# Macaron block, softmax attention: the causal mask moved from VectorE's minima to TensorE

## The chip, the cores and the metric

The kernel runs on one NeuronCore of one Trainium2 chip. The metric is the device time of one execution in microseconds (us), the median of several runs. One further execution was recorded by the hardware profiler, and all rows below come from it. A NeuronCore has TensorE (PE in the rows; PEld is its weight load), VectorE (DVE), ScalarE (ACT), GpSimd (POOL) and SyncE (SP), each with a queue of its own; they wait for each other by semaphores. TensorE writes only into PSUM, here eight banks of 512 fp32 columns over 128 partitions.

## What is computed

Two layers on x of shape (4, 1024, 128), each a half-weighted feed-forward part, an attention part and the feed-forward part again. The change touches the second layer's attention:

```python
D_K = 64
Q = jnp.einsum('bmd,hdk->bhmk', x, P_q)          # 16 heads
K = jnp.einsum('bmd,hdk->bhmk', x, P_k)
V = jnp.einsum('bmd,hdv->bhmv', x, P_v)
logits = jnp.einsum('bhmk,bhnk->bhmn', Q, K) * math.sqrt(D_K)
causal = jnp.tril(jnp.ones((m, m), dtype=bool))
logits = jnp.where(causal[None, None], logits, -jnp.inf)
key_weights = jax.nn.softmax(logits, axis=-1)
o = jnp.einsum('bhmm,bhmv->bhmv', key_weights, V)
y = jnp.einsum('bhmv,hdv->bmd', o, P_o)
```

The einsum with `mm` takes the diagonal of the weights alone. So for each head and query the kernel needs the masked row's extreme, the sum of the exponentials over the row, and the logit of the query with its own key.

## The kernel before

The program is a row of stages, each with its own code for the five engines. The stage here is `softmax_diagonal`. It runs over 32 units: unit `u` is head pair `u % 8` in batch `u // 8`. A unit has the scores of two heads, 1024 queries by up to 1024 keys. Queries go in eight tiles of 128; tile `q` needs keys 0 to `(q + 1) * 128` (`wide(q)`), so only its last 128 columns cross the diagonal. The tiles run in the order 1, 5, 6, 4, 2 (with 0), 3, 7 (`ORDER`, `LITTLE`).

**TensorE.** Q and K are split into a high and a low part, and each score is the sum of three products (`passes`). Head 0 of the pair lies on partitions 0 to 63, head 1 on 64 to 127, so a score matmul uses 64 rows of the array (`64*128` in the rows), and two of them, one for each head, can run beside each other. `big` (L2830) does the tiles of 640 to 1024 keys: for each head two halves of the keys in two banks, six matmuls a head, head 1's issued two steps behind head 0's (`SKEW`). `little` (L2855) does tiles 1, 2, 0 and 3 with one bank for a head. `diagonals` (L2845) sums the products of each query with its own key, with 128 rows and 32 columns of the array. `project` (L2808 to L2810) makes Q and K of the next unit, three matmuls of 128 rows for each of four halves; it stands ahead of tile 1 of the unit. The eight banks go round in order (`first_bank`); before a bank is written again, `wait_bank` waits until its last reader is done. So tile 4 waits for the exps of tile 5, tile 7 for those of tile 4.

**VectorE.** `lowest` (L2962) adds the mask to a tile's scores in PSUM, stores them back and takes their minimum (the scores are negated by the scale of -1 that the exp has) into `arg`, one instruction for each head and tile, each followed by a short one that reads the accumulator. It also copies Q's and K's second halves out of PSUM (`copy_out_dve`, L2891), adds up the diagonals (`add_own`), and at batch ends inverts, divides and copies (`invert`, `divide`, `keep`).

**ScalarE.** `exps` (L2942) does exp with the minimum as bias in place in PSUM and accumulates the sum; it also copies the first halves of Q and K (L2885).

**GpSimd** splits the copies into high and low parts and multiplies Q by K for the diagonals.

Semaphores: `scored` counts finished heads of tiles, `mx_done` minima, `exp_done` exps.

Of the kernel before, what the change touches and what calls it, by code (L numbers as in the profile page):

```python
# [17 lines left out]
BF16 = mybir.dt.bfloat16  # L18
I32 = mybir.dt.int32
U32 = mybir.dt.uint32  # L20
ALU = mybir.AluOpType
# [81 lines left out]
def build(nc, I, out):  # L103
# [41 lines left out]
    ident = sb("ident", [P, P], F32)  # L145
    before = sb("before", [P, P], BF16)
    onesb = sb("onesb", [P, P], BF16)
    cmask = sb("cmask", [P, SEQ], BF16)
    pair_ones = sb("pair_ones", [P, 3 * H1], F32)
    iota = sb("iota", [P, 32], F32)  # L150
    sel32 = sb("sel32", [P, E0], F32)
# [203 lines left out]
    def setup():  # L355
# [45 lines left out]
        def gpsimd(pool):  # L401
# [18 lines left out]
            select(before[:], [[1, P]], 0, -1, ALU.is_gt, 0.0)  # L420
            pool.memset(onesb[:], 1.0)
            then(pool.memset(cmask[:], 0.0))
            select(cmask[:, SEQ - P:], [[-1, P]], 0, 1, ALU.is_ge, MASKED)
            then(pool.memset(pair_ones[:], 0.0))
            then(pool.memset(pair_ones[:, H1:H1 + 2], 1.0))
            select(pair_ones[:, H1:H1 + 1], [[0, 1]], DK - 1, -1, ALU.is_ge, 0.0)
# [2229 lines left out]
    def softmax_diagonal(split, used):  # L2656
# [68 lines left out]
        def wait_bank(pe, k, freed, count):  # L2725

            if k in last_user:
                pe.wait_ge(*last_user[k])
            last_user[k] = (S[freed], count)

        def out_count(v, kind, half):
            mine = [k for k, h in PROJECT if h == half]
            return v * len(mine) + mine.index(kind) + 1

        def wait_out(pool, v, kind):

            pool.wait_ge(S["out_act"], out_count(v, kind, 0))
            pool.wait_ge(S["out_dve"], out_count(v, kind, 1))

        def copy_of(v, kind, half):  # L2740
            return (KF[v % 2] if kind == "k" else QF)[:, half * BLK:(half + 1) * BLK]
# [39 lines left out]
                project(pe, 1, k)  # L2781

        def open_out(pe):
            pe.wait_ge(S["out_act"], out_count(0, "q", 0))
            pe.wait_ge(S["out_dve"], out_count(0, "k", 1))

        def open_act(act):
            copy_out_act(act, 0)
# [10 lines left out]
        def project(pe, v, k):  # L2799
            kind, half = PROJECT[k]  # L2800
            g, b = which(v)
            wh, wl = (all_w[:, 2 * (kind == "k") + w, g * P:(g + 1) * P] for w in range(2))
            at = slice(b * SEQ + half * BLK, b * SEQ + (half + 1) * BLK)
            to = project_bank(v, k)
            if k == 0 and v < 2:
                pe.wait_ge(split["xl_done"], 2 if v == 0 else 4)
            wait_bank(pe, to, "out_dve" if half else "out_act", out_count(v, kind, half))
            pe.matmul(bank(to), wh, xl[:, at], start=True, stop=False)  # L2808
            pe.matmul(bank(to), wl, xh[:, at], start=False, stop=False)  # L2809
            pe.matmul(bank(to), wh, xh[:, at], start=False, stop=True).then_inc(S["projected"], 1)  # L2810

        def tensor(pe):
# [4 lines left out]
            def head(w, a, at, n):  # L2817
                return w[a * DK:(a + 1) * DK, at:at + n]

            def big(u, n):  # L2820
                q = ORDER[n]
                half = wide(q) // 2
                steps = [(p, k) for p in range(3) for k in range(2)]

                def step(a, m):
                    p, k = steps[m]
                    qs, ks = passes(u)[p]
                    if p == 0:
                        wait_bank(pe, (first_bank(u, n) + 2 * a + k) % BANKS, "exp_done", scored_before(u, n, a) + 1)
                    last = pe.matmul(big_scores(u, n, a)[:, k, :], head(qs, a, q * P, P),  # L2830
                                     head(ks, a, k * half, half), start=(p == 0), stop=(p == 2))
                    if m == len(steps) - 1:
                        last.then_inc(S["scored"], 1)

                for m in range(len(steps) + SKEW):
                    if m < len(steps):
                        step(0, m)
                    if m >= SKEW:
                        step(1, m - SKEW)
# [8 lines left out]

            def little(u, n):
                for a in range(2):  # L2850
                    wait_bank(pe, (first_bank(u, n) + a) % BANKS, "exp_done", scored_before(u, n, a) + 1)
                for q in LITTLE[ORDER[n]]:
                    for p, (qs, ks) in enumerate(passes(u)):
                        for a in range(2):
                            last = pe.matmul(small_scores(u, n, q, a), head(qs, a, q * P, P), head(ks, a, 0, wide(q)),  # L2855
                                             start=(p == 0), stop=(p == 2))
                            if p == 2 and q == LITTLE[ORDER[n]][-1] and q != DIAG:
                                last.then_inc(S["scored"], 1)
                if ORDER[n] == DIAG:
                    g, b = which(u)  # L2860
                    if g == 0 and b > 0:
                        last = turn_own(pe, b - 1, spare_of(u, 0))
                    last.then_inc(S["scored"], 1)
                    diagonals(u)
# [15 lines left out]

        def copy_out_act(act, v):
            for k, (kind, half) in enumerate(PROJECT):
                if half == 0:
                    wait_copy(act, v, k, kind)
                    act.activation(copy_of(v, kind, half), bank(project_bank(v, k)), ACT.Copy).then_inc(S["out_act"], 1)  # L2885

        def copy_out_dve(dve, v):
            for k, (kind, half) in enumerate(PROJECT):
                if half == 1:
                    wait_copy(dve, v, k, kind)  # L2890
                    dve.tensor_copy(copy_of(v, kind, half), bank(project_bank(v, k))).then_inc(S["out_dve"], 1)  # L2891

# [65 lines left out]
                        last.then_inc(S["exp_done"], 1)  # L2958
        def vector(dve):
            def lowest(u, q, a, src):  # L2960
                mask = cmask[:, SEQ - wide(q):].rearrange("p (k n) -> p k n", k=src.shape[1])
                return dve.tensor_tensor_reduce(src, src, mask, 1.0, 3e38, ALU.add, ALU.min, kept_at(arg, u, q, a))  # L2962

            def add_own(u):
                g, b = which(u)
# [9 lines left out]
            for u in range(UNITS):  # L2975
                if u < UNITS - 1:
                    copy_out_dve(dve, u + 1)
                for n, q in enumerate(ORDER):
                    done = u // PAIRS - 1
                    if done >= 0 and n == 1 and u % PAIRS == 0:  # L2980
                        invert(dve, done)
                    if done >= 0 and n == 1 and u % PAIRS == 1:
                        divide(dve, done)
                    if done >= 0 and n == 3 and u % PAIRS == 1:
                        keep(dve, done)
                    for a in range(2):
                        dve.wait_ge(S["scored"], scored_before(u, n, a) + 1)
                        if q == DIAG and a == 0 and u > 0 and u % PAIRS == 0:
                            arguments(dve, u // PAIRS - 1, spare_of(u, 0))
                        if q == DIAG and a == 1:  # L2990
                            add_own(u)
                        if q >= BT:
                            last = lowest(u, q, a, big_scores(u, n, a))
                        else:
                            for one in LITTLE[q]:
                                last = lowest(u, one, a, small_scores(u, n, one, a).unsqueeze(1))
                        last.then_inc(S["mx_done"], 1)

        opening = Opening(open_pe, open_act, open_dve, open_out, next_pe)
        closing = Beside(end_pe, end_act, end_dve)  # L3000
# [134 lines left out]
```

## Time and profile before

| | us |
|---|---|
| median of 3 runs (1689.14 to 1694.79) | 1689.76 |
| profiled execution | 1692.65 |
| its span, first to last instruction | 1690.5 |
| busy in it: TensorE | 1469.8 |
| VectorE | 1335.7 |
| ScalarE | 1022.8 |
| GpSimd | 861.6 |

Busy time is the union of an engine's instructions. Matmuls overlap each other in their pipeline, and the ends of matmuls are modelled, so distances between starts tell more of TensorE than durations. The chain of work that ended last is followed back from the last instruction, at each step to what released it; its rows give start, length and number of instructions. A timeline row gives start, length, engine, line, operation, output <- inputs with shapes, the number of instructions merged, and in brackets the idle time before it and what ended it.

### The profile page before, as it was taken

What the parts mean: (1) busy time and instruction counts of PE and PEld (TensorE: products, weight loads), DVE (VectorE), ACT (ScalarE), POOL (GpSimd) and SP (SyncE); (2) the same over time, 40 slices, a digit from 0 to 9 for tenths busy, and PEclk for the clock granted to TensorE, in tenths of its full rate; (3) what the DMA queues carried; (4) which work ended last, traced back from release to release, by engine and by line L of the source; (5) the groups of instructions that cost most, each with busy time, mean ns of one, the idle gap of its engine ahead of it and who ended that gap; (6) DMA issues with size and microseconds to landing.
All of it is one profiled execution on the core that took longest, in us unless ns stands there. A gap on an engine that the chain in (4) does not pass through costs nothing.

```text
span 1690.5 us, 30128 instructions
## 1 busy us (share of the span) xinstructions
PE 1469.8 (87%) x8653; PEld 1074.6 (64%) x8653; DVE 1335.7 (79%) x3816; ACT 1022.8 (61%) x2170; POOL 861.6 (51%) x743
## 2 busy tenths in 40 slices
PE   5999999898999994999549999999989899769990
PEld 4778877655666663777436676667666566457770
DVE  7599998567667675787679999999989767857876
ACT  7444432364223234888569999989989622268880
POOL 5756653210134333577656666656656225637673
PEclk9999998999999996999869999999989999879995
DMA  9990010000101004232199800000000001122225
GB/s 194 178 182 17 1 24 28 1 1 1 30 31 45 31 18 100 54 79 67 43 205 181 150 1 1 2 1 1 1 1 1 1 15 36 41 56 68 68 63 150
DMA packets 182171, 91.67 MB, mean 54 GB/s; under 512 B 43829, under 2 KB 176902, under 8 KB 182048
## 3 DMA queue, kind: packets, MB, share of 16 engines
q1 hardware_dynamic: 167840, 71.19, 23.1%
q0 software_dynamic: 9984, 16.89, 3.1%
q10 hardware_dynamic: 4224, 2.10, 0.4%
q8 instruction: 60, 0.98, 0.2%
q14 instruction: 63, 0.52, 0.1%
HBM read 32.59 MB, written 61.18 MB: 55 GB/s over the span
## 4 chain that ended last, share of the span: by engine, by line
PE 63%; DVE 14%; ACT 8%; issue 6%; DMA 3%; POOL 3%; DVEq 2%; SPq 1%; POOLq 0%; ACTq 0%
PE psum L1362 9%; PE psum L2830 7%; PE psum L658 5%; PE psum L2855 5%; PE psum L659 4%; PE psum L660 4%; ACT psum L2942 4%; DVE psum L2962 3%; PE psum L2808 2%; PE psum L2809 2%; PE psum L2810 2%; PE psum L1121 1%; PE psum L190 1%; PE psum L1123 1%; PE psum L1122 1%
## 5 line engine op out<-in xcount | busy, mean ns | idle before, releaser
L2942 ACT ACTIVATE psum<-psum,gate 128x128 f32<-128x128 f32 (+7 forms) x512 | 368.1, 727 | 39.8 <-DVE gate L2962 37.9
L2962 DVE CUSTOM_DVE_ANT_0 psum<-psum,cmask 128x128 f32<-128x128 f32 (+7 forms) x512 | 371.3, 790 | 16.3 <-PE psum L2830 11.7
L2440 POOL DMA_INDIRECT answers<-ed,answer_to x184 | 202.5, 1101 | 80.2 <-issue 43.7
L1362 PE MATMUL psum<-raw_all,w 128*128 128x512 f32 x384 | 195.4, 592 | 1.5 <-DVE raw_all L1490 1.5
L658 PE MATMUL psum<-xl,wreg 128*128 128x512 f32 x320 | 182.0, 569 | 2.8 <-ACT psum L2942 1.5
L1488 DVE SCALAR_TENSOR_TENSOR raw_all<-psum,hg 128x512 f32<-128x512 f32 x128 | 88.1, 690 | 67.3 <-PE psum L660 64.5
L2830 PE MATMUL psum<-spare_sets_room 64*128 64x384 f32 (+3 forms) x768 | 115.3, 369 | 16.2 <-ACT psum L2942 16.2
L659 PE MATMUL psum<-xh,wreg 128*128 128x512 f32 x320 | 126.9, 396 | 0.0
L660 PE MATMUL psum<-xh,wreg 128*128 128x512 f32 x320 | 126.5, 395 | 0.0
L2830 PE MATMUL psum<-hh,hl 64*128 64x384 f32 (+3 forms) x768 | 113.1, 376 | 13.4 <-ACT psum L2942 13.4
L2830 PEld LDWEIGHTS psum<-spare_sets_room 64*128 64x128 f32 x768 | 85.9, 185 | 45.3 <-ACT psum L2942 39.3
L2830 PEld LDWEIGHTS psum<-hh,hl 64*128 64x128 f32 x768 | 87.9, 194 | 39.0 <-ACT psum L2942 32.3
L2356 DVE TENSOR_TENSOR hl<-gate,hh 128x512 fp32r<-128x512 f32 x92 | 63.4, 690 | 59.3 <-ACT hh L2318 36.9
L2942 ACT ACTIVATION_READ_ACCUMULATOR psum<-psum,gate 128x1 f32 x512 | 110.2, 215 | 0.0
L1235 POOL TENSOR_TENSOR hl<-hg,hh 128x512 fp32r<-128x512 f32 x65 | 85.9, 1324 | 47.5 <-ACT hh L1167 46.6
L819 POOL DMA_INDIRECT rows<-raw_all,row_no x64 | 61.7, 965 | 78.5 <-PE psum L660 63.8
L819 POOL DMA_INDIRECT rows<-row,row_no x64 | 62.0, 968 | 69.1 <-PE psum L660 52.1
L1167 ACT ACTIVATE hh<-hg 128x512 fp32r<-128x512 f32 x86 | 54.1, 633 | 67.1 <-DVE hg L1198 65.2
L201 POOL TENSOR_TENSOR spare_p<-spare_p 128x1 f32<-128x1 f32 x63 | 19.5, 309 | 134.6 <-DVE row_no L780 64.0
L658 PEld LDWEIGHTS psum<-xl,wreg 128*128 128x128 f32 x320 | 61.3, 192 | 39.2 <-issue 27.6
L1362 PEld LDWEIGHTS psum<-raw_all,w 128*128 128x128 f32 x384 | 72.1, 189 | 19.9 <-DVE raw_all L1490 2.1
L659 PEld LDWEIGHTS psum<-xh,wreg 128*128 128x128 f32 x320 | 61.5, 192 | 32.2 <-issue 27.7
(432 smaller groups left out, 4073.3 us busy)
## 6 DMA issues: line engine op xcount, KB each, us to landing
rows<-blank SPq DMA_DIRECT2D x146, 258.0 KB, 7.3
row<-rows SPq DMA_DIRECT2D x46, 256.0 KB
raw_all<-answers SPq DMA_DIRECT2D x32, 256.0 KB, 4.7
w<-in_L_ffn_W_dram SPq DMA_DIRECT2D x16, 256.0 KB, 3.1
answers<-ed,answer_to POOLq DMA_INDIRECT x184
x<-in_L_attn_x_dram SPq DMA_DIRECT2D x4, 512.0 KB, 6.1
out_dram<-x ACTq DMA_DIRECT2D x8, 256.0 KB, 4.7
rawD<-in_L_ffn_values_dram SPq DMA_DIRECT2D x4, 256.0 KB, 6.9
```

Of the source, the lines that this page charges most:

```text
L658: pe.matmul(dst, wh, xl[:, blk(i)], start=start, stop=False)
L659: pe.matmul(dst, wl, xh[:, blk(i)], start=False, stop=False)
L660: return pe.matmul(dst, wh, xh[:, blk(i)], start=False, stop=stop)
L819: pool.indirect_dma_start(rows, bass.IndirectOffsetOnAxis(ap=row_no[:, i % 2, c, t:t + 1], axis=0), row_of(i)[:, t, c, :], None).then_inc( ...
L1235: pool.tensor_tensor(hl[:, j % SLOTS, :], kept[n % len(kept)], hh[:, j % SLOTS, :].bitcast(F32), ALU.subtract).then_inc(S["lo_pool"], 1)
L1362: pe.matmul(bank(B_OUT[i % 2]), col(dn, j), hidden[:, n % HID, :], start=(j == 0), stop=(j == nf - 1)).then_inc(S["dn_done"], 1)
L1488: last = dve.scalar_tensor_tensor(out, raw, 0.0, gates_now, ALU.max, ALU.mult)
L2440: pool.indirect_dma_start(answers, bass.IndirectOffsetOnAxis(ap=answer_to[:, out.odd, t:t + 1], axis=0), y_row[:, out.odd, t, :], None, bo ...
L2830: last = pe.matmul(big_scores(u, n, a)[:, k, :], head(qs, a, q * P, P), head(ks, a, k * half, half), start=(p == 0), stop=(p == 2))
L2855: last = pe.matmul(small_scores(u, n, q, a), head(qs, a, q * P, P), head(ks, a, 0, wide(q)), start=(p == 0), stop=(p == 2))
L2942: return act.activation(src, src, ACT.Exp, bias=kept_at(arg, u, q, a), scale=-1.0, accum_out=kept_at(esum, u, q, a))
L2962: return dve.tensor_tensor_reduce(src, src, mask, 1.0, 3e38, ALU.add, ALU.min, kept_at(arg, u, q, a))
```

## The change

The mask becomes a 128x128 bf16 tile, and a bf16 identity `ident16` is made beside it. TensorE adds the mask: `hide` multiplies the identity by the mask and accumulates into the 128 diagonal columns of the scores, ahead of the last matmul that writes there. That is once for each head and tile, 16 times a unit, with all 128 rows of the array. VectorE's `lowest` becomes a plain minimum that writes nothing back; for tiles 1, 2, 0 and 3 one instruction (`lowest_two`) takes the minima of both heads, after waiting for both. Three of the four halves of Q and K are copied by VectorE, and K's first half alone by ScalarE (`BY_ACT`). Waits follow: `wait_bank` is given the semaphore itself, and `wait_out` waits for both halves.

```diff
-    cmask = sb("cmask", [P, SEQ], BF16)
+    cmask = sb("cmask", [P, P], BF16)
+    ident16 = sb("ident16", [P, P], BF16)
...
-            select(cmask[:, SEQ - P:], [[-1, P]], 0, 1, ALU.is_ge, MASKED)
+            select(cmask[:], [[-1, P]], 0, 1, ALU.is_ge, MASKED)
+            then(pool.tensor_copy(ident16[:], ident[:]))
...
+        BY_ACT = (("k", 0),)
+
+        def out_sem(kind, half):
+            return S["out_act" if (kind, half) in BY_ACT else "out_dve"]
...
-            pool.wait_ge(S["out_act"], out_count(v, kind, 0))
-            pool.wait_ge(S["out_dve"], out_count(v, kind, 1))
+            for half in range(2):
+                e.wait_ge(out_sem(kind, half), out_count(v, kind, half))
...
+            def hide(diagonal):
+
+                pe.matmul(diagonal, ident16[:], cmask[:], start=False, stop=False, skip_group_check=True)
+
             def big(u, n):
...
                     qs, ks = passes(u)[p]
+                    if (p, k) == (2, 1):
+                        hide(big_scores(u, n, a)[:, 1, half - P:half])
...
                     for p, (qs, ks) in enumerate(passes(u)):
+                        if p == 2:
+                            for a in range(2):
+                                hide(small_scores(u, n, q, a)[:, wide(q) - P:])
                         for a in range(2):
...
-                if half == 0:
+                if (kind, half) in BY_ACT:
...
             def lowest(u, q, a, src):
-                mask = cmask[:, SEQ - wide(q):].rearrange("p (k n) -> p k n", k=src.shape[1])
-                return dve.tensor_tensor_reduce(src, src, mask, 1.0, 3e38, ALU.add, ALU.min, kept_at(arg, u, q, a))
+                return dve.tensor_reduce(kept_at(arg, u, q, a), src, AX.XY, ALU.min)
+
+            def lowest_two(u, n, q):
+                g, b = which(u)
+                at = 3 * P if q == 0 else 0
+                src = psum[:, first_bank(u, n):first_bank(u, n) + 2, at:at + wide(q)]
+                return dve.tensor_reduce(arg[:, b * QT + q, 2 * g:2 * g + 2], src, AX.X, ALU.min)
...
-                    for a in range(2):
-                        dve.wait_ge(S["scored"], scored_before(u, n, a) + 1)
-                        if q == DIAG and a == 0 and u > 0 and u % PAIRS == 0:
-                            arguments(dve, u // PAIRS - 1, spare_of(u, 0))
-                        if q == DIAG and a == 1:
-                            add_own(u)
-                        if q >= BT:
-                            last = lowest(u, q, a, big_scores(u, n, a))
-                        else:
-                            for one in LITTLE[q]:
-                                last = lowest(u, one, a, small_scores(u, n, one, a).unsqueeze(1))
-                        last.then_inc(S["mx_done"], 1)
+                    if q >= BT:
+                        for a in range(2):
+                            dve.wait_ge(S["scored"], scored_before(u, n, a) + 1)
+                            lowest(u, q, a, big_scores(u, n, a)).then_inc(S["mx_done"], 1)
+                        continue
+                    dve.wait_ge(S["scored"], scored_before(u, n, 0) + 1)
+                    if q == DIAG and u > 0 and u % PAIRS == 0:
+                        arguments(dve, u // PAIRS - 1, spare_of(u, 0))
+                    dve.wait_ge(S["scored"], scored_before(u, n, 1) + 1)
+                    if q == DIAG:
+                        add_own(u)
+                    for one in LITTLE[q]:
+                        last = lowest_two(u, n, one)
+                    last.then_inc(S["mx_done"], 2)
```

On TensorE's queue, tile 1, the diagonals and tiles 5, 6 and 4 of one unit stood so in the kernel before (the name, the output and inputs, and the output's shape; L2855 is `little`, L2845 the diagonals, L2830 `big`):

```order
L2855 MATMUL psum<-hh,hl 128x256 x6
L2845 MATMUL psum<-ed,pair_ones 32x256 x4
L2830 MATMUL psum<-hh,hl 128x384 x12
L2830 MATMUL psum<-hh,hl 128x448 x12
L2830 MATMUL psum<-hh,hl 128x320 x12
```

And tile 1, the diagonals and tiles 5 and 6 in the changed kernel, where L2829 is `hide`, L2871 `little`, L2858 the diagonals and L2843 `big`:

```order
L2871 MATMUL psum<-hh,hl 128x256 x4
L2829 MATMUL psum<-cmask,ident 128x128 x2
L2871 MATMUL psum<-hh,hl 128x256 x2
L2858 MATMUL psum<-ed,pair_ones 32x256 x4
L2843 MATMUL psum<-hh,hl 128x384 x8
L2829 MATMUL psum<-cmask,ident 128x128
L2843 MATMUL psum<-hh,hl 128x384 x3
L2829 MATMUL psum<-cmask,ident 128x128
L2843 MATMUL psum<-hh,hl 128x384
L2843 MATMUL psum<-hh,hl 128x448 x8
L2829 MATMUL psum<-cmask,ident 128x128
L2843 MATMUL psum<-hh,hl 128x448 x3
```

In the narrow tile the two mask products stand together ahead of the last pair; in a wide tile they stand after eight and after eleven of the twelve score matmuls.

On VectorE's queue, from the copies to tile 5, one unit before (ISA is the masked minimum, with its accumulator read behind it):

```order
L2891 COPY hg<-psum 128x512
L2891 COPY row<-psum 128x512
L2962 ISA psum,gate<-psum,cmask 128x256
L2962 ISA gate 128x1
L2972 TENSOR_TENSOR own<-psum,own 128x256
L2962 ISA psum,gate<-psum,cmask 128x256
L2962 ISA gate 128x1
L2962 ISA psum,gate<-psum,cmask 128x2x384
```

And in the changed kernel the whole turn of a unit:

```order
L2907 COPY hg<-psum 128x512
L2907 COPY row<-psum 128x512
L2907 COPY hg<-psum 128x512
L2993 TENSOR_TENSOR own<-psum,own 128x256
L2983 TENSOR_REDUCE gate<-psum 128x2
L2977 TENSOR_REDUCE gate<-psum 128x1 x6
L2983 TENSOR_REDUCE gate<-psum 128x2 x3
L2977 TENSOR_REDUCE gate<-psum 128x1 x2
```

A third copy stands ahead of the minima, the diagonals' sum goes ahead of tile 1's minimum, and tile 1 has one minimum in place of two.

## Rows read from the trace of the kernel before

**Rows 1.** The page, chain that ended last, by engine.
```profile
PE 63%; DVE 14%; ACT 8%; issue 6%; DMA 3%; POOL 3%; DVEq 2%; SPq 1%; POOLq 0%; ACTq 0%
```
**Rows 2.** Busy by stretch: length, PE, PEld, DVE, ACT, POOL, clock, DMA, GB/s.
```profile
1054.30:1068.07 13.77, 12.90 (x97) 9.57 (x93) 13.25 (x36) 12.87 (x36) 9.15 (x5) 1.00 0.01 2
885.00:1325.00 440.00, 406.90 (x2853) 304.40 (x2849) 419.22 (x1094) 400.11 (x1054) 282.41 (x155) 0.97 0.21 33
```
**Rows 3.** The chain in one unit: start us, us, what.
```profile
1054.37 1.25 PE psum L2830 x12
...
1055.64 0.97 DVE psum L2962
...
1056.70 1.91 ACT psum L2942 x4
...
1058.66 1.14 PE psum L2830 x9
...
1064.08 0.43 PE psum L2808
...
1067.02 0.55 PE psum L2855 x6
...
1068.13 0.37 PE psum L2830
```
**Rows 4.** Timeline of TensorE, tile 4's first matmuls, a unit earlier.
```profile
1043.97 0.70 PE L2830 MATMUL psum<-spare_sets_room 64*128 64x320 f32 x3 [0.55 <-ACT psum L2942]
```
**Rows 5.** Timeline of TensorE around changes of form.
```profile
1052.63 0.39 PE L2809 MATMUL psum<-xh,wreg 128*128 128x512 f32 x1
1052.86 0.39 PE L2810 MATMUL psum<-xh,wreg 128*128 128x512 f32 x1
1053.18 0.39 PE L2855 MATMUL psum<-hh,hl 64*128 64x256 f32 x2
...
1053.52 0.28 PE L2855 MATMUL psum<-hh,hl 64*128 64x256 f32 x2
1053.73 0.41 PE L2845 MATMUL psum<-ed,pair_ones 128*32 128x256 f32 x2
...
1063.70 0.38 PE L2830 MATMUL psum<-hh,hl 64*128 64x512 f32 x1
1064.01 0.50 PE L2808 MATMUL psum<-xl,wreg 128*128 128x512 f32 x1
```
**Rows 6.** VectorE by line and shape: count, busy us, mean ns, idle before.
```profile
L2962 DVE DVE_READ_ACCUMULATOR2_ANT gate<- 128x1 f32 x512 | 72.1, 141 | 0.0
L2962 DVE CUSTOM_DVE_ANT_0 psum<-psum,cmask 128x512 f32<-128x512 f32 x64 | 44.1, 731 | 0.0
L2891 DVE COPY hg<-psum 128x512 f32<-128x512 f32 x31 | 21.2, 685 | 0.0
...
L1794 DVE TENSOR_REDUCE k_sum<-raw_all 128x64 f32<-128x512 f32 x8 | 5.5, 686 | 0.5
L847 DVE TENSOR_REDUCE hg<-hg 128x32 f32<-128x256 f32 x2 | 0.8, 420 | 0.1
```
**Rows 7.** Timeline of VectorE, tile 7's two minima.
```profile
1050.16 1.26 DVE L2962 CUSTOM_DVE_ANT_0 psum<-psum,cmask 128x1024 f32<-128x1024 f32 x1
...
1051.34 1.26 DVE L2962 CUSTOM_DVE_ANT_0 psum<-psum,cmask 128x1024 f32<-128x1024 f32 x1
```
**Rows 8.** Timeline of TensorE in a later stage, bf16 matmuls and a load.
```profile
1403.35 0.10 PEld L1394 LDWEIGHTS psum<-m,onesb 128*128 128x128 bf16 x1 [0.33 <-issue]
...
1403.35 0.19 PE L1394 MATMUL psum<-m,before 128*128 128x64 bf16 x1
1403.38 0.20 PE L1394 MATMUL psum<-m,onesb 128*128 128x64 bf16 x1
```
**Rows 9.** The chain around a batch end: tile 5 of four units.
```profile
982.44 1.25 PE psum L2830 x12
...
1026.83 1.25 PE psum L2830 x12
```

More of the change, by code:

```diff
@@ L2728, in wait_bank, with wait_out @@
                 pe.wait_ge(*last_user[k])
-            last_user[k] = (S[freed], count)
+            last_user[k] = (freed, count)
+        BY_ACT = (("k", 0),)
+        def out_sem(kind, half):
+            return S["out_act" if (kind, half) in BY_ACT else "out_dve"]
         def out_count(v, kind, half):
-            mine = [k for k, h in PROJECT if h == half]
-            return v * len(mine) + mine.index(kind) + 1
-        def wait_out(pool, v, kind):
-            pool.wait_ge(S["out_act"], out_count(v, kind, 0))
-            pool.wait_ge(S["out_dve"], out_count(v, kind, 1))
+            mine = [one for one in PROJECT if (one in BY_ACT) == ((kind, half) in BY_ACT)]
+            return v * len(mine) + mine.index((kind, half)) + 1
+        def wait_out(e, v, kind):
+            for half in range(2):
+                e.wait_ge(out_sem(kind, half), out_count(v, kind, half))
         def copy_of(v, kind, half):
@@ L2783, in open_out @@
         def open_out(pe):
-            pe.wait_ge(S["out_act"], out_count(0, "q", 0))
-            pe.wait_ge(S["out_dve"], out_count(0, "k", 1))
+            wait_out(pe, 0, "k")
+            wait_out(pe, 0, "q")
         def open_act(act):
@@ L2806, in project @@
                 pe.wait_ge(split["xl_done"], 2 if v == 0 else 4)
-            wait_bank(pe, to, "out_dve" if half else "out_act", out_count(v, kind, half))
+            wait_bank(pe, to, out_sem(kind, half), out_count(v, kind, half))
             pe.matmul(bank(to), wh, xl[:, at], start=True, stop=False)
@@ L2827, in step @@
                     qs, ks = passes(u)[p]
+                    if (p, k) == (2, 1):
+                        hide(big_scores(u, n, a)[:, 1, half - P:half])
                     if p == 0:
-                        wait_bank(pe, (first_bank(u, n) + 2 * a + k) % BANKS, "exp_done", scored_before(u, n, a) + 1)
+                        wait_bank(pe, (first_bank(u, n) + 2 * a + k) % BANKS, S["exp_done"], scored_before(u, n, a) + 1)
                     last = pe.matmul(big_scores(u, n, a)[:, k, :], head(qs, a, q * P, P),
@@ L2850, in little @@
                 for a in range(2):
-                    wait_bank(pe, (first_bank(u, n) + a) % BANKS, "exp_done", scored_before(u, n, a) + 1)
+                    wait_bank(pe, (first_bank(u, n) + a) % BANKS, S["exp_done"], scored_before(u, n, a) + 1)
                 for q in LITTLE[ORDER[n]]:
                     for p, (qs, ks) in enumerate(passes(u)):
+                        if p == 2:
+                            for a in range(2):
+                                hide(small_scores(u, n, q, a)[:, wide(q) - P:])
                         for a in range(2):
@@ L2888, in copy_out_dve @@
             for k, (kind, half) in enumerate(PROJECT):
-                if half == 1:
+                if (kind, half) not in BY_ACT:
                     wait_copy(dve, v, k, kind)
```

## The prediction

> **What bounds the kernel now.** I read the page first, then the busy time of the engines in the softmax stage, then the chain of work that ended last in one unit, then TensorE's single matmuls. The page gives TensorE 63% of the chain and VectorE 14% [rows 1], too coarse to judge one stage. The stage that the change edits runs from about 885 to 1325 us: 32 units (head pair times batch) in which TensorE is busy 407 of 440 us, VectorE 419 and ScalarE 400 [rows 2]. Three engines look full at once, so the busy shares don't tell which one sets the time.
>
> The chain over one unit does [rows 3]: 384-wide halves of query tile 5 on TensorE (1.25 us), VectorE's minimum (0.97), ScalarE's exps of both heads (1.91), then TensorE alone: from 1058.66 tile 4, tiles 2, 0, 3 and tile 7, from 1064.08 to 1067.02 twelve projection matmuls, then tile 1, the diagonals, and at 1068.13 tile 5 of the next unit. From tile 5 to tile 5 (1054.37 to 1068.13) a unit lasts 13.76 us. Only tile 6 is off the chain, since TensorE runs it while VectorE and ScalarE work on tile 5. About 10.8 of the 13.8 us of the chain are TensorE's (13.76 less 0.97 and 1.91, and 0.1 between them). VectorE itself is at 13.25 of 13.77 us [rows 2]. So the chain and VectorE's own queue are nearly the same length, and anything put on TensorE outside tile 6 lengthens the chain at once.
>
> How much could TensorE take? Tile 4's matmuls wait for the exps of tile 5: three start after 0.55 us of idle time (1043.97, a unit of 13.77 earlier; so 1057.74 here) [rows 4], and the other nine at 1058.66 [rows 3]. Summing TensorE without waits: projections 2.94, tile 1 and the diagonals 1.11 (1067.02 to 1068.13), tile 5 1.15 (its 1.25 less the modelled end) [rows 3]; the others at 0.23 us per 512 columns (1052.63 to 1052.86 [rows 5]), the two heads side by side: tile 6 1.2, tile 4 0.87, tiles 2, 0 and 3 0.52, 0.33 and 0.69, tile 7 1.38, and 0.1 before the next projections: 10.3 us. So TensorE stands idle or half used for about 3.5 us of a unit.
>
> **The change, part by part.**
>
> (a) *VectorE's wide tiles* lose the added mask and the store. The custom instruction takes 1.26 us for 1024 elements [rows 7] and 731 ns for 512 [rows 6], about 200 ns plus 1.04 ns an element. A plain reduction isn't shown at these shapes from PSUM; the nearest rows are 686 ns for 512 and 420 for 256 elements in SBUF, so about 155 plus 1.04 [rows 6]. That is 45 ns less, eight times a unit: 0.36 us. Bounds: nothing saved, to 0.14 us each if the accumulator read behind each one (141 ns [rows 6]) was never overlapped; it mostly is, and I take 45.
>
> (b) *Narrow tiles*: eight instructions become four of double width. The elements stay; 8 x 0.20 less 4 x 0.155 is 0.98 us, less the 0.08 by which neighbours overlap (1050.16 to 1051.34 is 1.18 us for an instruction of 1.26 [rows 7]), four times: about 0.65.
>
> (c) *Copies*: VectorE takes the third one, 685 ns less the overlap, so 0.6 us more [rows 6, 7]; ScalarE loses about as much. Together VectorE goes from 13.3 to about 12.9 us a unit, ScalarE from 12.9 to 12.3. If VectorE alone set the pace the stage would gain 0.4 x 32 = 13 us.
>
> (d) *The mask on TensorE*: 16 matmuls of 128 columns a unit. The columns alone are small: bf16 matmuls of 64 columns start 0.03 us apart on this clock [rows 8], so 0.055 for 128. But the scores are computed in 64-row halves (64*128 in the rows), two heads beside each other, and the identity product needs all 128 rows. The rows show what it costs to pass between these forms. Within the projections a start follows a start by 0.23 us; from the last projection (1052.86) to the first 64-row matmul (1053.18) it is 0.32; tile 7's last matmul to the next projection 1063.70 to 1064.01, 0.31. Tile 1 (256 columns, 0.115) to the diagonals (128*32) is 1053.52 to 1053.73, 0.21 [rows 5]. So 0.09 us at each change of form, while 128*128 matmuls of different lines pass without it. On top, the first matmul after a change shows its weight load: 0.39 against 0.28 us for the same 256 columns [rows 5], so 0.11. The identity's load is bf16; such a load takes 0.10 us [rows 8], and the two bf16 matmuls, each with its own, start 0.03 apart: I take 0.03 of it as exposed.
>
> One identity product between 64-row matmuls therefore costs 0.09 + 0.03 + 0.055 + 0.09 + 0.11 = 0.37 us. In the wide tiles both products of a tile stand apart: 8 x 0.37 = 3.0 us. In the narrow ones the two stand together, 0.43 a pair, four pairs: 1.7.
>
> The Trainium skill states both sides of this. TensorEngine Tiling, section Key Properties: changing the tiling mode drains the engine; the trace agrees, with the 0.09 us. TensorE: Matmul & The Clock Gate, section Back-to-back issue gap, gives about 81 ns for a 128-column matmul with its load in a stream, and by that the sixteen would be an estimated 1.3 us a unit; that is the first rival below in another form.
>
> (e) *The order in the wide tiles.* Today the two heads' six matmuls each run side by side: twelve in 1.25 us [rows 3] are six pitches of 0.17. In the new order head 0's product comes when head 1 has issued three of six, and nothing passes a full-array product. Head 1 then runs two matmuls alone: eight pitches in place of six. Two pitches more are 0.35, 0.41, 0.29 and 0.47 us for tiles 5, 6, 4 and 7: 1.5 us.
>
> (f) *Waits.* The narrow minimum now waits for both heads, so ScalarE's exp of head 0 starts later; for tile 1 also behind the diagonals. Behind this wait on VectorE stands tile 5's minimum, and VectorE has 0.5 us of a unit to spare today [rows 2]. In the new timing the wait lies under TensorE's work. Removing the store has no price. The set-up on GpSimd gets one copy and a shorter fill; it is under 1 us of 1690 and I take it as nothing.
>
> **Sum.** TensorE without waits: 10.3 + 3.0 + 1.7 + 1.5 = 16.5 us a unit. Does it then still wait? From head 0's end in tile 5 to tile 4's start TensorE has 0.17 + 0.37 + 0.17 of tile 5 and 8 x 0.2 + 0.74 of tile 6: 3.05 us. The way through VectorE and ScalarE takes 2.1 (1055.64 to 1057.74 [rows 3, 4]). So the wait for the exps is gone, and TensorE's own work is the bound. I find no other wait over 0.2 us. The unit goes from 13.77 to about 16.5, so 2.73 x 32 = 87 us. Against it: at each of three batch ends VectorE's extra work (reciprocal, division, a copy) now makes three units last 44.4 us (982.44 to 1026.83 [rows 9]) where 41.3 are regular, 3.1 more; with VectorE 3.6 us below TensorE most of it hides, and I take back 7 of the 9 us. Net +80 us. The profiled execution took 1692.65 us, 1690.5 of it span; its 2.15 us around the span stay. It lies 2.9 above the median of 1689.76; I add the 80 to the median: **1770 us**.
>
> **Rivals.**
>
> *1. The products stream without the change of form.* Each costs its columns or its load, 0.055 to 0.11 us. For it: no row shows a single full-array product between halves. Against it: the 0.09 at every change. TensorE's sum is then 10.3 + 1.5 + 0.9 to 1.8, 12.7 to 13.6, under a unit. The chain holds 14 of the 16 (all but tile 6's), so it grows by 0.8 to 1.5 us, of which VectorE's relief and the remaining waits give part back: +0.3 to +0.9 a unit, 10 to 29 us: 1700 to 1719. Chance 0.09.
>
> *2. The drain overlaps partly*, say half of the 0.31 us that isn't columns: a product costs 0.2, a pair 0.26; TensorE needs 10.3 + 1.6 + 1.0 + 1.5 = 14.4, and the chain, which waits again, about 15.2: +1.1 to +1.5 a unit less 5, so 1720 to 1735. Chance 0.09.
>
> *3. Not slower.* The products fall into TensorE's 3.5 idle us and the unit follows VectorE, 0.4 shorter: 1690 - 13 = 1677, or 1690 where the chain holds its 13.76. It decides below a price that the chain doesn't feel: 14 products cost as little as what (a) and the shared minimum take off the chain, about 0.2 us, so under 0.02 us each, less than their own columns. For it only the idle time; against it that this lies at tile 4 and the products elsewhere. Chance 0.04 (0.02 faster, 0.02 within).
>
> *4. Worse than the sum.* The granted clock is 0.97 over the stage [rows 2]; stretches at half clock partly hide in waits today and would not then; pairs may also expose a second load. Plus 0.5 to 1 us a unit: 1786 to 1802. Chance 0.13.
>
> **Numbers.** Forecast (1750 to 1786) 0.65, rivals 0.09, 0.09, 0.04, 0.13. The range 1725 to 1800 leaves out rivals 1 and 3 and the edges of 2 and 4. A measurement of this kernel tells 0.3% (5 us) from no change: faster 0.02, within 0.3% 0.02, slower 0.96.
>
> **What would show it.** Right: a unit of about 16.5 us in the chain; TensorE nearly the whole chain of the stage, with no wait for ScalarE before tile 4; each identity product starting about 0.2 us after its predecessor's start plus columns, and the next 64-row matmul showing a long first load; tile 7 lasting about 2.6 us; VectorE idle for over 3 us a unit, waiting for scores; reductions of 1024 elements near 1.22 us. Wrong: products 0.06 to 0.1 us apart from their neighbours (rival 1); VectorE still full at a unit of 16 us, which would mean that a reduction from PSUM costs far more than one from SBUF; ScalarE's exps of tile 1 late enough to hold tile 6.

## The result and the profile after

| | before | changed |
|---|---|---|
| median, us (4 runs each) | 1691.71 (1689.14 to 1694.79) | 1781.13 (1765.77 to 1781.97) |
| ratio, 95% interval | | 1.0506 (1.0446 to 1.0567) |
| span of the profiled execution, us | 1690.5 | 1779.2 |
| busy TensorE, VectorE, ScalarE, us | 1469.8, 1335.7, 1022.8 | 1589.1, 1335.5, 1011.1 |

The change costs 5.1%: 1781 us against a forecast of 1770 and a range of 1725 to 1800. (The kernel before has one run more in this table than in the one ahead of the forecast.)

The busy time of the engines in the changed kernel, first in one regular unit from tile 1 to tile 1, then over the stage; the columns are those of [rows 2]:

```profile
1054.51:1070.73 16.22, 16.22 (x109) 10.36 (x109) 13.11 (x16) 11.69 (x31) 9.01 (x5) 1.00 0.01 2
880.00:1411.00 531.00, 529.38 (x3343) 335.17 (x3339) 420.22 (x507) 388.87 (x1024) 281.74 (x155) 0.94 0.17 28
```

TensorE is busy the whole 16.22 us. VectorE's 13.11 here is about what it had in [rows 2], though its busy share is now 81%: it has room, and the room buys nothing. The chain of work that ended last says the same; here are some parts of one unit (start us, us, what; L2871 is `little`, L2829 the mask products, L2858 the diagonals, L2843 `big`):

```profile
1055.54 0.57 PE psum L2858 x8
1056.11 1.09 PE psum L2843 x7
...
1058.07 1.21 PE psum L2843 x9
...
1071.77 0.57 PE psum L2858 x8
```

No VectorE or ScalarE row stands between the two rows of the diagonals, where [rows 3] has 0.97 and 1.91 us of them. Diagonals to diagonals is 16.23 us.

TensorE's timeline from tile 5 to tile 4 of that unit shows where it goes:

```profile
1056.04 1.16 PE L2843 MATMUL psum<-hh,hl 64*128 64x384 f32 x8
1057.13 0.23 PE L2829 MATMUL psum<-cmask,ident 128*128 128x128 bf16 x1
1057.29 0.62 PE L2843 MATMUL psum<-hh,hl 64*128 64x384 f32 x3
1057.84 0.23 PE L2829 MATMUL psum<-cmask,ident 128*128 128x128 bf16 x1
1058.00 1.28 PE L2843 MATMUL psum<-hh,hl 64*128 64x384 f32 x9
1059.22 0.23 PE L2829 MATMUL psum<-cmask,ident 128*128 128x128 bf16 x1
...
1060.14 1.25 PE L2843 MATMUL psum<-hh,hl 64*128 64x448 f32 x9
1061.32 0.23 PE L2829 MATMUL psum<-cmask,ident 128*128 128x128 bf16 x1
```

From product to product in tile 5 is 0.71 us and holds two pitches of 0.175 (a pitch is the distance from one score matmul to the next that doesn't run beside it); what is left, 0.36 us, is the price of one product with the change of form to it and back. Product to next matmul is 0.16 (1057.13 to 1057.29, 1057.84 to 1058.00). The single matmuls of this trace give the other two parts: from the lone matmul at 1056.86 to the product at 1057.13 is 0.27 us, 0.09 over its pitch, and from the first matmul behind the product (1057.29) to the next (1057.57) is 0.28, 0.11 over it. The three parts are 0.09, 0.16 and 0.11; the forecast had 0.09, 0.175 and 0.11.

VectorE's reductions, by line and shape (columns as in [rows 6]):

```profile
L2977 DVE TENSOR_REDUCE gate<-psum 128x1 f32<-128x1024 f32 x64 | 75.7, 1221 | 17.8 <-PE psum L2843 17.3
L2983 DVE TENSOR_REDUCE gate<-psum 128x2 f32<-128x512 f32 x32 | 21.8, 680 | 0.0
L2993 DVE TENSOR_TENSOR own<-psum,own 128x256 f32<-128x256 f32 x28 | 11.9, 425 | 25.2 <-PE psum L2858 25.2
```

1221 ns for 1024 elements and 680 for 512: a plain reduction from PSUM costs what [rows 6] gave for SBUF, 686 ns for 512 and, by their slope, 1.22 us for 1024. The idle time ahead of the diagonals' sum (25.2 us) is VectorE waiting for TensorE.

### The profile page after: what moved, and what is told of

Its sections match the earlier page's. It is cut to its first block, busy times and chain, and to the rows that moved or that the text cites. A ratio compares the mean times of both kernels' runs of the same rounds, so it can differ in the third digit from the quotient of the medians.

```text
span 1779.2 us, 30579 instructions
## 1 busy us (share of the span) xinstructions
PE 1589.1 (89%) x9165; PEld 1100.7 (62%) x9165; DVE 1335.5 (75%) x3208; ACT 1011.1 (57%) x2138; POOL 861.8 (48%) x744
## 4 chain that ended last, share of the span: by engine, by line
PE 73%; DVE 8%; issue 5%; DMA 5%; ACT 4%; POOL 3%; SPq 1%; DVEq 0%; POOLq 0%; ACTq 0%
PE psum L2843 14%; PE psum L1364 9%; PE psum L2871 5%; PE psum L660 4%; PE psum L661 4%; PE psum L662 4%; PE psum L2829 4%; PE psum L2815 2%; DMA answers<-ed,answer_to 2%; PE psum L2816 2%; PE psum L2817 2%; PE psum L2266 2%; PE psum L2268 2%; PE psum L2267 2%; DMA row<-rows 1%
## 5 line engine op out<-in xcount | busy, mean ns | idle before, releaser
L2977 DVE TENSOR_REDUCE gate<-psum 128x1 f32<-128x768 f32 (+3 forms) x256 | 249.4, 1019 | 42.8 <-PE psum L2843 41.5
L2843 PE MATMUL psum<-spare_sets_room 64*128 64x384 f32 (+3 forms) x768 | 145.1, 403 | 1.6 <-ACT psum L2958 1.6
L2843 PE MATMUL psum<-hh,hl 64*128 64x384 f32 (+3 forms) x768 | 140.8, 399 | 0.0
L1490 DVE SCALAR_TENSOR_TENSOR raw_all<-psum,hg 128x512 f32<-128x512 f32 x128 | 88.1, 690 | 66.5 <-PE psum L662 63.8
L2983 DVE TENSOR_REDUCE gate<-psum 128x2 f32<-128x512 f32 (+3 forms) x128 | 99.7, 818 | 29.6 <-PE psum L2871 29.6
L2958 ACT ACTIVATION_READ_ACCUMULATOR psum<-psum,gate 128x1 f32 x512 | 105.6, 206 | 0.0
L2829 PEld LDWEIGHTS psum<-cmask,ident 128*128 128x128 bf16 x512 | 39.4, 97 | 103.3 <-issue 96.6
L2843 PEld LDWEIGHTS psum<-spare_sets_room 64*128 64x128 f32 x768 | 85.9, 192 | 24.5 <-issue 6.2
L2829 PE MATMUL psum<-cmask,ident 128*128 128x128 bf16 x512 | 97.5, 232 | 0.0
L2843 PEld LDWEIGHTS psum<-hh,hl 64*128 64x128 f32 x768 | 84.2, 191 | 21.2 <-issue 6.6
```

What stands on the lines that cost most here:

```text
L2829: pe.matmul(diagonal, ident16[:], cmask[:], start=False, stop=False, skip_group_check=True)
L2958: return act.activation(src, src, ACT.Exp, bias=kept_at(arg, u, q, a), scale=-1.0, accum_out=kept_at(esum, u, q, a))
L2977: return dve.tensor_reduce(kept_at(arg, u, q, a), src, AX.XY, ALU.min)
L2983: return dve.tensor_reduce(arg[:, b * QT + q, 2 * g:2 * g + 2], src, AX.X, ALU.min)
```

## Experiments

The experiments ran on chips on which the kernel before took 1706.5 us (e1 to e4) and 1710.7 us (e5 to e8), so they are compared by their ratio to it. A unit is measured in the chain from diagonals to diagonals.

### e1: the changed kernel without the mask products

```diff
             def hide(diagonal):
-                pe.matmul(diagonal, ident16[:], cmask[:], start=False, stop=False, skip_group_check=True)
+                return
```

> The changed kernel without its sixteen mask products (the mask is left out of the computation; all else of the change stays: plain minima, two heads in one narrow minimum, three copies on VectorE). My theory, that the products are the whole loss: a unit returns to 13.4 to 13.8 us and the time to 1677 to 1692 us, since VectorE's relief of about 0.4 us a unit counts only while the chain lets it. Rival, that the plain reductions from PSUM, the third copy or the wait for both heads cost something of their own: the time stays above 1700 us.

Ratio 0.9971 (0.9937 to 1.0005), 1702.5 us. Two regular units in its chain:

```profile
940.15 0.57 PE psum L2858 x8
...
953.84 0.57 PE psum L2858 x8
```

13.69 us a unit, 0.08 less than before. So the whole loss of a regular unit comes with the products, and plain minima, shared narrow minima and the third copy, which take 0.4 us a unit from VectorE, give back 0.08. The first theory holds by the unit; the rival that VectorE's part costs something there falls. In time, 1702.5 against 1706.5 us is at the edge of what the runs can tell. It is above the 1692 that I named as the upper end, and above the rival's 1700 too, but so is the kernel before on this chip; times the 1691.7 us of the first chip the ratio gives 1687. At the batch ends VectorE's part isn't free: the second unit after each lasts 18.5 us here, where two of the three in the trace of the kernel before last 15.4 and 15.5.

### e2: the kernel before with the products and nothing else

```diff
+                    if (p, k) == (2, 1):
+                        hide(big_scores(u, n, a)[:, 1, half - P:half])
...
+                        if p == 2:
+                            for a in range(2):
+                                hide(small_scores(u, n, q, a)[:, wide(q) - P:])
```

> The kernel before with the sixteen identity products added and nothing else of the change (VectorE adds the mask once more, which leaves the result as it is). My theory: TensorE sets the time and VectorE's work doesn't matter, so a unit is 16.2 us as in the changed kernel and the time 1770 to 1790 us. Rival, that the changed VectorE work has a part in the loss: the time is nearer to 1740 us. Rival, that VectorE's relief hides a part of the products' cost: it is above 1795 us.

Ratio 1.0529 (1.0511 to 1.0546), 1796.0 us. That is the changed kernel's own ratio within its interval, reached without any of its VectorE work. Busy time in 80 us of regular units:

```profile
920.00:1000.00 80.00, 80.00 (x533) 50.96 (x531) 66.51 (x174) 65.21 (x168) 43.10 (x25) 1.00 0.66 109
```

TensorE 80.00 of 80, VectorE 66.5. The absolute time lies above the 1770 to 1790 that I named, and 1 us above the second rival's 1795; the kernel before is 0.9% slower on this chip too, and times the first chip's 1691.7 the ratio gives 1781. A regular unit is 16.34 us in this trace, 0.11 more than in the changed kernel. So the second rival is right in kind but small: VectorE's relief hides about 0.1 us of a unit, as in e1, some 3 us of the kernel. e1 and e2 together leave the products as the cause of the loss.

### e3: heads in step, both products of a tile together

```diff
-        SKEW = 2
+        SKEW = 0
...
-                    if (p, k) == (2, 1):
-                        hide(big_scores(u, n, a)[:, 1, half - P:half])
+                    if (p, k) == (2, 1) and a == 0:
+                        for one in range(2):
+                            hide(big_scores(u, n, one)[:, 1, half - P:half])
```

> The changed kernel with the two heads of a wide tile issued in step (SKEW 0) and both mask products together ahead of the last pair: eight changes of form fewer, and no matmul that runs alone. By my sum TensorE needs 10.3 + 8 x 0.43 = 13.7 us a unit in place of 16.5; then the chain through VectorE and ScalarE binds again with seven of the eight pairs of products on it (13.76 + 3.0 less 0.3 to 1.5): 15.3 to 16.3 us a unit, 1735 to 1770 us. Rival, that the products cost by their number and not by where they stand: no change from 1781 us.

Ratio 1.0399 (1.0378 to 1.0421), 1774.4 us, with the same sixteen products. A unit is 15.90 us:

```profile
951.67 0.57 PE psum L2859 x8
...
967.57 0.55 PE psum L2859 x5
```

That is inside 15.3 to 16.3; in time 1774 is 4 us over what I named, on the slower chip. Against e2, on the same chip, it gains 22 us: about 13 in the regular units and 9 in the first unit of the stage, which lasts 17.4 us here and 26.6 there, with the granted clock at 0.50 for 6.8 and for 27.3 us. TensorE's timeline at tiles 6 and 4 shows that the bound has moved back to the exps:

```profile
1072.12 0.28 PE L2829 MATMUL psum<-cmask,ident 128*128 128x128 bf16 x2
1072.33 0.70 PE L2844 MATMUL psum<-spare_sets_room 64*128 64x448 f32 x3
1073.49 0.99 PE L2844 MATMUL psum<-spare_sets_room 64*128 64x320 f32 x9 [0.47 <-ACT psum L2959]
```

The pair costs 0.21 us from its first product to the next matmul, against 0.16 for a lone one, so the second product adds 0.05. TensorE now waits 0.47 us before tile 4. The products on the chain cost even where TensorE has time to spare elsewhere; where they stand matters, but not enough.

### e4: the mask in the 64-row form

Each product is split into two of 64 rows on the partitions of its head, so that no change of form is left within the scores. `ident2` and `cmask2` hold the other half's rows.

```diff
+            then(pool.memset(ident2[:], 0.0))
+            select(ident2[:], [[-1, P]], DK, 1, ALU.not_equal, 1.0)
+            select(ident2[:], [[-1, P]], -DK, 1, ALU.not_equal, 1.0)
+            then(pool.memset(cmask2[:], MASKED))
+            select(cmask2[:], [[0, P]], -DK, 1, ALU.is_ge, 0.0)
+            select(cmask2[:], [[1, P]], DK, -1, ALU.is_gt, 0.0)
+            select(cmask2[:], [[-1, P]], DK, 1, ALU.is_ge, MASKED)
...
-            def hide(diagonal):
-                pe.matmul(diagonal, ident16[:], cmask[:], start=False, stop=False, skip_group_check=True)
+            def hide(diagonal, a):
+                rows = slice(a * DK, (a + 1) * DK)
+                for one, mask in ((ident16, cmask), (ident2, cmask2)):
+                    pe.matmul(diagonal, one[rows, :], mask[rows, :], start=False, stop=False, skip_group_check=True)
```

> The changed kernel with each mask product split in two of 64 rows each, on the partitions of its head, so that TensorE never leaves the 64-row form within the scores: 32 products in place of 16, in the places of before. My theory, that the change of form and the order that it forces are the cost: a unit falls from 16.24 to 14.0 to 14.4 us, the time to 1695 to 1712 us. Rival, that a product costs by its number, its bf16 type or its write into PSUM: twice as many cost at least as much, 1781 us or more.

Ratio 1.0073 (1.0050 to 1.0096), 1718.8 us: 32 products in place of 16 cost 0.7% in place of 5.1%. (1718.8 is over the 1695 to 1712 that I named; times the first chip's 1691.7 the ratio gives 1704.) The unit in its chain, and tile 7's products in its timeline (L2839 the products, L2853 `big`):

```profile
947.55 0.57 PE psum L2868 x8
...
961.92 0.57 PE psum L2868 x8
```

```profile
1059.82 0.39 PE L2853 MATMUL psum<-spare_sets_room 64*128 64x512 f32 x1
1059.82 0.28 PE L2839 MATMUL psum<-cmask,ident 64*128 64x128 bf16 x2
1059.92 0.53 PE L2853 MATMUL psum<-spare_sets_room 64*128 64x512 f32 x2
```

14.37 us a unit, inside 14.0 to 14.4. The two products start together with the other head's score matmul and the next one follows 0.10 us later. The rival (cost by number, by type or by the write into PSUM) falls: twice the products, a seventh of the loss. What is left against e1, 0.68 us a unit, lies in tiles 5, 2, 3 and 1, by the starts of the tiles in the two traces: 0.16 to 0.19 us each. Tiles 6, 4, 0 and 7 with the projections behind them are no longer than in e1, or by 0.02 us at most.

### e7: each product of the wide tiles twice

```diff
-                        hide(big_scores(u, n, a)[:, 1, half - P:half])
+                        for _ in range(2):
+                            hide(big_scores(u, n, a)[:, 1, half - P:half])
```

> The changed kernel with each mask product of the wide tiles issued twice in a row (masked scores get the mask twice, the result is the same): eight products a unit more, no change of form more. My theory, that of a product's 0.36 us only 0.055 are its columns and the rest the two changes of form: a unit grows by 0.45 to 0.6 us, from 16.24 to 16.7 to 16.85. Rival, that each product costs 0.3 us or more wherever it stands: 18.6 us and over.

This kernel ran once, in 1800.5 us, and wasn't timed beside the others, so only its unit counts:

```profile
1085.56 0.57 PE psum L2859 x8
...
1102.08 0.57 PE psum L2859 x8
```

16.52 us, 0.29 more for eight products, less than the 0.45 to 0.6 I named and far from 18.6. In the timeline the second product adds the 0.05 us expected (1103.65 to 1103.86 is 0.21):

```profile
1103.65 0.28 PE L2829 MATMUL psum<-cmask,ident 128*128 128x128 bf16 x2
1103.86 0.62 PE L2844 MATMUL psum<-hh,hl 64*128 64x384 f32 x3
```

Eight times 0.05 would be 0.4. The rest is a wait that it fills, in tile 4. From its first matmul to its first product are 1.18 us in the changed kernel (1060.14 to 1061.32 above) and 1.01 here:

```profile
1106.88 1.08 PE L2844 MATMUL psum<-hh,hl 64*128 64x448 f32 x9
1107.89 0.29 PE L2829 MATMUL psum<-cmask,ident 128*128 128x128 bf16 x2
```

Tile 4 is the narrowest of the wide tiles, and yet in the changed kernel this part is nearly as long as in tile 6 (1058.00 to 1059.22, 1.22 us). What it waits for are head 1's exps of tile 5: the read of their sum ends at 1060.64, and head 1's first load of tile 4 starts at 1060.69. ScalarE's row and TensorE's, in the changed kernel:

```profile
1060.44 0.20 ACT L2958 ACTIVATION_READ_ACCUMULATOR psum<-psum,gate 128x1 f32 x1
```

```profile
1060.69 0.18 PEld L2843 LDWEIGHTS psum<-hh,hl 64*128 64x128 f32 x1
```

The view of the waits shows another one, 0.24 us ahead of the projections in 25 units of the changed kernel and in 4 of e7, but it costs nothing: from tile 7's last matmul to the first projection are 0.42 us in the one and 0.43 in the other.

### e5 and e8: the division moved, and the changed kernel again

In the changed kernel the second unit after each batch end is far longer than the others. Its diagonals, with those of the unit ahead:

```profile
1015.92 0.57 PE psum L2858 x8
1032.32 0.61 PE psum L2858 x8
1055.54 0.57 PE psum L2858 x8
```

16.40 and then 23.22 us. Three rows of the chain and three of the stretches tell what lies in it:

```profile
1034.03 1.75 DVE gate L2923
1035.78 0.88 DVE gate L2977
...
1036.68 1.88 ACT psum L2958 x4
```

```profile
1032.00:1036.00 4.00, 4.00 (x33) 2.47 (x33) 3.07 (x5) 1.10 (x5) 3.77 (x3) 1.00 0.01 2
1036.00:1040.00 4.00, 3.47 (x20) 2.03 (x19) 4.00 (x5) 3.32 (x7) 3.92 (x3) 1.00 0.00 0
...
1044.00:1048.00 4.00, 4.00 (x18) 2.55 (x16) 1.76 (x3) 3.38 (x12) 0.00 (x0) 0.50 0.00 0
```

VectorE's division (L2923) stands ahead of tile 5's minimum, TensorE waits for the exps behind it, and a few us later the granted clock is 0.50, the lower of its two levels (1.2 in place of 2.4 GHz), until about 1054. e5 moves the division and the copy behind it:

```diff
-                    if done >= 0 and n == 1 and u % PAIRS == 1:
+                    if done >= 0 and n == 4 and u % PAIRS == 1:
                         divide(dve, done)
-                    if done >= 0 and n == 3 and u % PAIRS == 1:
+                    if done >= 0 and n == 6 and u % PAIRS == 1:
                         keep(dve, done)
```

> The changed kernel with VectorE's division moved from ahead of tile 5's minima to ahead of tile 2's, and the copy behind it (keep) from ahead of tile 4's minima to ahead of tile 7's, in the second unit after each batch end. In the changed kernel that unit lasts 23.1 to 24.6 us in place of 16.24: the division takes 1.83 us, TensorE waits, and 4 us later the granted clock is 0.50 for 13.7 us. My theory, that this wait is what the slow clock follows: the unit falls to 16.3 to 17.5 us, the clock stays near 1.00 there, and the kernel is 15 to 21 us under the changed one run beside it. Rival, that the slow clock comes with the batch end's transposes or with TensorE's drains whatever VectorE does: the unit stays over 20 us and the time within 6 us of the changed kernel.

> The changed kernel as it is, on the same chip as the run before it, so that the two can be compared, and to see whether the half-clock stretches behind the batch ends come again. All theories: 1.045 to 1.057 of the kernel before; mine: three units of over 20 us, each with a stretch at clock 0.50.

e5: ratio 1.0379 (1.0329 to 1.0429), 1778.8 us. e8: ratio 1.0476 (1.0434 to 1.0518), 1792.4 us. The difference is 13.6 us, a little under the 15 to 21 named. e5's unit is regular (1045.70 to 1061.98), and its clock stays at 1.00:

```profile
1045.70 0.57 PE psum L2858 x8
1061.98 0.57 PE psum L2858 x8
```

```profile
1048.00:1052.00 4.00, 4.00 (x29) 2.73 (x28) 3.71 (x4) 3.18 (x8) 3.92 (x3) 1.00 0.00 0
```

The same holds at the other two batch ends: no stretch at 0.50 lies between 914 and 1415 us of e5's trace. Of e8's claim of three units over 20 us, each with a stretch at 0.50, two came true (23.3 us with 13.7 us of it, 20.2 with 6.8). The third lasted 18.0 us: the same wait, and no stretch at all. In e7, too, the wait stands at all three batch ends, with units of 18.0 us, and the clock stays up. The third unit of e8 and the first of e7:

```profile
1314.00:1331.00 17.00, 16.47 (x100) 10.24 (x98) 16.50 (x18) 12.48 (x33) 8.22 (x5) 1.00 0.01 1
```

```profile
1050.97:1068.95 17.98, 17.80 (x119) 10.81 (x117) 16.42 (x18) 12.60 (x33) 9.03 (x6) 1.00 0.00 1
```

So the division in its old place costs a wait of about 1.7 us each time (17.95 against 16.24), and moving it takes that away: this is shown. The lower clock came behind that wait at three of three batch ends of the changed kernel and of e3, at two of three of e8 and of e2, and at none of e7; without the wait, in e5, at none of three. That the wait brings it on is likely by these counts, but not shown, and no run here tells why it comes once and not the next time. What it costs, e8 tells: against its third unit, 2.2 us more for 6.8 us at half clock and 5.3 more for 13.7.

### e6: the same moves in the kernel before

The diff is that of e5, on the kernel before.

> The kernel before with the same two moves of division and copy as in e5. VectorE is full there, so what is taken from one place comes back in another: my theory says within 3 us of the kernel before, with the three units behind a batch end at 14.5 to 15.5 us. Rival, that the moves also save TensorE's wait of 1.8 us and its half-clock stretch of 3.4 us: 5 to 8 us faster than before, which would be a version better than both.

Ratio 0.9960 (0.9938 to 0.9982), 1702.3 us in 10 runs, against 1710.7. My theory ("within 3 us", units of 14.5 to 15.5) falls and the rival's 5 to 8 us hold: it is about 7 us faster than the kernel before, by a little more than the 0.3% that a measurement tells, and so the fastest version here that keeps the mask. The unit that held the division and the copy is 14.00 us long (before it was 1010.82 to 1026.26, 15.44):

```profile
1011.00 0.57 PE psum L2845 x8
1025.00 0.57 PE psum L2845 x8
```

The other two are 14.05 and 14.10 us (before 15.48 and 18.68). TensorE's wait of 1.8 us behind the copy is gone from all three, and the first two are shorter by 1.4 us each. The rival's other half isn't shown: the 3.4 us at half clock of the trace of before lie one unit ahead of the moved instructions (1003.1 and 1115.8), so their absence in e6 isn't the moves' work; the 6.8 us in the third unit (from 1248.9, behind the wait) may be. What I had missed stands in the last section: the copy was long only because GpSimd was at work.

## Why the prediction held, step by step

**Direction, bound and place.** Right. The step that carried it is (d): the 0.09 us at each change of form, read from three places of the trace of before [rows 5], applies to the mask products as well. The price came out at 0.36 us against 0.37, and part by part too (0.09, 0.16, 0.11). Tile 7 lasts 2.66 us where I named 2.6 as a sign. e2 shows that the products alone make the loss, e4 that it is the 128-row form and the order it forces, e7 that another product without another change of form adds 0.05.

**The unit.** 16.23 us against 16.5, by two misses of opposite sign. The step that was too large is (e), two lone pitches in each of four wide tiles. At the end of tiles 5 and 6 head 1's last matmul runs beside the first of the next tile: the row at 1058.00 above holds nine matmuls, one of tile 5 and eight of tile 6. From start to start tiles 5 and 6 last 1.96 and 2.13 us where my terms give 2.24 and 2.35, 0.5 less together. The step that was too small is in the sum: "the wait for the exps is gone". I had followed head 0 alone, and for it that is right. Head 1's first matmul of tile 4 still waits for head 1's exps of tile 5, about 0.2 us (the two rows in e7), and tile 4 lasts 2.11 us where my terms give 1.90.

**VectorE.** The reductions (a) and (b) cost what I took, 1221 ns forecast as 1.22 us. That this would be worth next to nothing was right too: 0.1 us a unit by e1 and e2, and 0.3% of the time in e1, with an interval that reaches no change.

**Batch ends.** Wrong by 18 us, and hidden in part by the shorter unit, which gives 9 back; that 1770 came as near to 1781 as it did is partly luck. I took back 7 of 9 us, since VectorE had room. From the starts of the diagonals, the units around the three batch ends together last 24 us more than regular ones in the changed kernel, and 13 us more in the kernel before: 11 us more, not 7 less. (The 9 were three times the first batch end; the third is longer, with a unit of 18.7 us.) The room was there over the unit but not at the place: the division stood right ahead of the one minimum on which the chain hangs, a wait of 1.7 us each, and behind it came 13.7, 13.7 and 17.1 us at half clock. That is rival 4 in its mechanism, at three places. The first unit of the stage belongs here too: 23.0 us, with 17.1 at the clock's lower level, where before it was 15.1, with 3 of them. The regular units give 31 x 2.46 = 76 us, the batch ends 11 and the first unit 5 beyond its share; these 92 are the 91.6 by which the stage is longer (530.9 against 439.2, from the first diagonals to the last). These stretches differ from one execution to the next; one of the four timed runs of the changed kernel took 1765.77 us, at a mean granted clock of 0.948 where the other three had 0.939 to 0.941.

**Rival 1** (products stream) and **rival 3** (not slower) are excluded by the 0.36 us in the timeline. **Rival 2** (half the drain overlaps) had 0.2 us for a product and a unit of 15.2, and is excluded by the same rows.

## What to carry to other kernels

Before a matmul is added to TensorE, look at the form (rows*columns) of its neighbours in the queue: with a form of its own it pays for two changes and stops what runs side by side, here over six times its own length (0.36 us against 0.055). The same operand cut to the neighbours' form cost a seventh in the whole, with twice the instructions. And where a small step of VectorE stands ahead of the one result that TensorE waits for, move it behind, and to where GpSimd rests.

## What I had not expected of the hardware

**VectorE held by GpSimd.** VectorE's division and copy in SBUF last very differently with the same shapes. In the kernel before the copy overlaps a GpSimd instruction; the two rows are VectorE's and GpSimd's:

```profile
1016.56 1.98 DVE L2911 COPY gate<-gate 128x128 f32<-128x128 f32 x1
```

```profile
1016.09 2.37 POOL L2760 TENSOR_TENSOR hl<-hg,hl 128x1024 fp32r<-128x1024 f32 x1
```

Both end near 1018.5. In e6 the copy starts 0.47 us after GpSimd's last instruction and takes 0.21 us:

```profile
1021.46 0.21 DVE L2911 COPY gate<-gate 128x128 f32<-128x128 f32 x1
```

```profile
1018.55 2.44 POOL L2762 TENSOR_TENSOR ed<-hg,r 128x1024 f32<-128x1024 f32 x1
```

The changed kernel's division, 1.83 us against 0.58 before, overlaps GpSimd in the same way. Away from GpSimd the same division takes 0.28 us (the last one of each trace). Wherever one of the two overlaps a GpSimd instruction that started first, it ends just behind it: the division 0.14 or 0.15 us after, the copy 0.08 or 0.09, in the traces of before, of the changed kernel and of e1 to e8 alike. The Trainium skill, SBUF — State Buffer, section SBUF: two separate sides, says that VectorE (in a two-port mode, or with two inputs in SBUF) and GpSimd take a shared port pair under an exclusive lock, and that the one that starts first holds it for its whole instruction; the trace agrees, with 1.98 against 0.21 us. Minima that read PSUM don't show it: tile 5's average 949 ns over 64, what 768 elements cost by the lengths of the other reductions. Nor does the reciprocal, with one input in SBUF: 0.94 to 0.95 us beside GpSimd and away from it.

**The clock after a short wait.** The wait behind the division leaves 0.82 us between two starts on TensorE where the work is 0.2 us, and the granted clock then stayed at 0.50 for 13.7, 13.7 and 17.1 us in the changed kernel; in e8, behind the same 0.82 us, for 13.7, 6.8 and 0. In the kernel before, the waits behind the copy leave 1.76, 1.81 and 1.80 us between two starts; the first two were followed by no stretch at the lower level, the third by one of 6.8 us. So the longer wait isn't the worse one. The runs don't show what makes the difference.
